# Two single-byte clears on GpSimd behind every row gather of an edge-attention kernel

## The reference

```python
K, Q, V = typed_linear(x, Wk), typed_linear(x, Wq), typed_linear(x, Wv)   # 192 wide, weights by node type
def edge_msgs(Kn, Qn, Vn, ek, eq):
    k = concat([Kn, ek]).reshape(-1, 4, 56);  q = concat([Qn, eq]).reshape(-1, 4, 56)
    att = einsum('ehd,ed->eh', k, q.sum(axis=1)) / sqrt(56)
    return att, concat([Vn, ek]).reshape(-1, 4, 56)
att, v     = edge_msgs(K[row], Q[col], V[row], e1, e2)      # pass o = 0, edges sorted by destination
att_i, v_i = edge_msgs(K[col], Q[row], V[col], e2, e1)      # pass o = 1, edges sorted by source
att, att_i = seg_softmax(att, col), seg_softmax(att_i, row)
agg = segment_sum([v * att, e0], col) + segment_sum([v_i * att_i, e0], row)
```

## Time and profile before

| | us |
|---|---|
| median of 3 runs (lowest to highest) | 4512.24 (4508.96 to 4513.65) |
| the profiled execution | 4514.77 |
| its span in the trace | 4513.0 |
| score pass 0, first gather to last product (L1436) | 1998.13 to 2696.44 |
| score pass 1, first gather to last product (L1436) | 3066.69 to 3773.75 |
| POOL busy over the whole span | 2876.4 (64%) |
| PE, DVE, ACT busy | 63%, 53%, 38% |

### The profile page before, as it was taken

How to read it: one execution, slowest core, us unless ns; L and a number is a source line. 1 busy time by engine, 2 the same in 40 slices (tenths; PEclk the granted TensorE clock), 3 DMA queues, 4 the chain that set the end, 5 groups by cost and what they waited for, 6 DMA issues and landing times.

```text
span 4513.0 us, 51523 instructions
## 1 busy us (share of the span) xinstructions
PE 2845.5 (63%) x13735; PEld 1923.5 (43%) x13735; DVE 2409.3 (53%) x5005; ACT 1721.4 (38%) x4345; POOL 2876.4 (64%) x2661
## 2 busy tenths in 40 slices
PE   4200005545473990767777778996777777996698
PEld 1000003333362660224444447884444445885455
DVE  6434434444451114336777775556777776665353
ACT  2222310000021112125555556774555555885451
POOL 4777776666667887665555557996555553555640
PEclk5555556777785995777777778997777778997798
DMA  5444449333345653677676676777887765664300
GB/s 163 134 136 127 141 116 245 91 93 93 89 90 191 196 183 101 212 220 215 202 212 207 203 191 163 204 193 190 208 210 208 209 203 141 173 173 131 102 1 29
DMA packets 805880, 720.83 MB, mean 160 GB/s; under 512 B 424290, under 2 KB 700364, under 8 KB 805469
## 3 DMA queue, kind: packets, MB, share of 16 engines
q1 hardware_dynamic: 645116, 399.08, 31.1%
q0 software_dynamic: 153536, 315.11, 25.1%
q10 hardware_dynamic: 6944, 3.34, 0.3%
HBM read 482.09 MB, written 241.99 MB: 160 GB/s over the span
## 4 chain that ended last, share of the span: by engine, by line
DVE 20%; POOL 16%; another core or an unknown queue 12%; PE 12%; issue 9%; ACT 7%; DVEq 4%; ACTq 2%; DMA 1%; SPq 1%; POOLq 0%
POOL rec_src L564 9%; DVE META L1423 7%; POOL AR L1661 4%; DVE BIGR L648 3%; DVE AR L1443 3%; ACT AR L1717 2%; DVEq L1439 2%; DVE AR L639 2%; DVE AR L1436 2%; ACT AR L1719 1%; ACT AR L1547 1%; PE ps L1822 1%; PE ps L2433 1%; ACTq L1718 1%
## 5 line engine op out<-in xcount | busy, mean ns | idle before, releaser
L1392 POOL DMA_INDIRECT AR<-kv_tab,META x832 | 791.0, 951 | 599.8 <-DVE AR L1436 337.0
L536 POOL DMA_INDIRECT rec_dst<-AR,slot_e x400 | 484.6, 1211 | 166.7 <-issue 166.4
L1423 DVE TENSOR_REDUCE META<-ps 128x8 f32<-128x1024 f32 x416 | 507.7, 1221 | 97.9 <-remote 57.7
L668 PE MATMUL ps<-AR 128*128 128x256 f32 x832 | 305.6, 532 | 362.4 <-issue 151.0
L622 POOL DMA_INDIRECT AR<-xn_tab,META x416 | 397.9, 956 | 199.7 <-issue 128.6
L1661 POOL TENSOR_TENSOR AR<-AR 128x896 f32<-128x896 f32 x208 | 352.1, 1693 | 233.3 <-ACT AR L1726 230.4
L1626 DVE TENSOR_TENSOR BIGR<-BIGR,ps 128x260 f32 x832 | 353.6, 425 | 228.9 <-PE ps L1700 144.6
L1700 PE MATMUL ps<-AR 128*128 128x260 f32 x1664 | 419.5, 395 | 11.3 <-POOL AR L1661 5.4
L1521 PE MATMUL ps<-AR,identb 128*128 128x512 bf16 x832 | 405.4, 487 | 15.4 <-issue 8.5
L564 POOL DMA_INDIRECT rec_src<-AR,slot_e x290 | 351.8, 1213 | 91.8 <-issue 88.3
L668 PEld LDWEIGHTS ps<-AR 128*128 128x128 f32 x832 | 212.8, 268 | 456.1 <-issue 262.3
(11 more groups left out here) (432 smaller groups left out, 5815.7 us busy)
## 6 DMA issues: line engine op xcount, KB each, us to landing
v_dst<-AR SPq DMA_DIRECT2D x104, 384.0 KB
AR<-v_dst SPq DMA_DIRECT2D x104, 384.0 KB
v_src<-AR SPq DMA_DIRECT2D x104, 384.0 KB
AR<-v_src SPq DMA_DIRECT2D x104, 384.0 KB
AR<-in_W_qvk SPq DMA_DIRECT2D x44, 608.0 KB
rec_raw<-AR SPq DMA_DIRECT2D x40, 640.0 KB, 3.3
AR<-rec_dst SPq DMA_DIRECT2D x104, 192.0 KB
AR<-rec_src SPq DMA_DIRECT2D x104, 192.0 KB
```

Source lines behind the costliest of these rows:

```text
L536: pool.indirect_dma_start(rec_tab[0], bass.IndirectOffsetOnAxis(ap=slot_e[0][0:EP, c * CC + k:c * CC + k + 1].bitcast(U32), axis=0), RD[s] ...
L668: ins = pe.matmul(l0_ps(s, u), OW[s][:, u, :], GA[s][:, u, :], start=True, stop=True)
L1392: pool.indirect_dma_start(KVR[s][:, u, 0:KV], None, kv_tab, bass.IndirectOffsetOnAxis(ap=META[o][:, g * U + u, 0:1].bitcast(U32), axis=0)) ...
L1423: ve.tensor_reduce(BMALL[o][:, g * U + 2 * half:g * U + 2 * half + 2, :].rearrange("p b h -> p (b h)"), PSA[:, 2048 + 1024 * half:3072 + 1 ...
```

## The change

Behind each of the 416 gathers of a pass POOL now executes two `memset` instructions, each of which writes a zero into one column of one byte on all 128 partitions of a new tile `PAD` (128 x 832 bytes). Gather b writes columns 2b and 2b+1, so no column is written twice within a pass. Nothing reads `PAD`. A `drain` closes the function. The rest of the kernel is unchanged, and all four other engines have the same instruction lists as before.

```diff
@@ -108,6 +108,7 @@
         ttype = sb("ttype", [1, TT], I32)
+        PAD = sb("PAD", [P, 832], mybir.dt.uint8)
@@ -1392,6 +1393,10 @@
                     pool.indirect_dma_start(KVR[s][:, u, 0:KV], None, kv_tab,
                                             bass.IndirectOffsetOnAxis(ap=META[o][:, g * U + u, 0:1].bitcast(U32), axis=0)
                                             ).then_inc(sem(f"rows{s}"), 16)
+                    for k in range(2):
+                        b = 2 * (g * U + u) + k
+                        pool.memset(PAD[:, b:b + 1], 0.0)
+            pool.drain()
```

## The result

The changed kernel took 4530.06 us (median of 7 runs, 4522.87 to 4533.44) against 4512.24 us of the kernel before; the ratio is **1.0031, 95% interval [1.0016, 1.0045]** (the quotient of the two medians, 1.0039, lies within it). One of the seven executions of the kernel before that ran beside it took 5703.81 us and is not part of the ratio. The forecast was 4350 us, faster. The profiled execution took 4523.49 us, its span is 4521.8 us.

The account below looks back on a forecast made before the run. The score passes were taken as bound by a loop: lagging gathers delay PE's signals, so product and slots are late and POOL stops. 4514.8 - 186 (no late signals) + 20 (pauses) = 4349, said as 4350 us; range 4285 to 4605.

Parts of the forecast that it names:

- x: Time the two clears add from one POOL gather to the next: taken as 0.16 us, ends -0.03 and 0.26.
- the sum: Score passes: 6.65 - 5.7 = 0.95 us saved per group, some 196 of 208 groups, 186 us; 20 us of pauses off.
- edge: Gathers issued every 1.26 us, worked off every 1.41: the backlog grows 0.15 us each unless x makes up the difference.
- lag: Gathers worked off more slowly than POOL issues them, 0.15 us more behind each; PE's signals held back after five or six.
- rate of 1.41 us: Time per gather at which gathers are worked off, against 1.26 us at issue; gathers 1.42 us apart would avoid late signals.
- Rival 1 with 4: Score passes: blocks of eight stay and POOL's idle time hides the clears, 4505 to 4523 us; chance 0.13, rival 4 included.
- rival 4: Clears run beside the gather, gathers stay 1.26 us apart, no change in time; counted within the joint chance of 0.13.
- Rival 2: Score passes: block stays, its end hangs on the last gather; 4600 us at x = 0.16, 4525 at 0.06; chance 0.22.
- Rival 3: Clears cost more than any row says, POOL becomes the bound from x = 0.41; 4700 us at x = 0.62; chance 0.10.

Follow-up runs that it names:

- 260 columns: Changed kernel with one 260-column clear behind each gather instead of two single-column clears, no closing drain: 4395.56 us, 0.9724 of the kernel before.
- 130 columns: Changed kernel with one 130-column clear behind each gather instead of two single-column clears, no closing drain: 4490.85 us, 0.9946 of the kernel before.
- clears at the end: Changed kernel with its 1664 clears and two drains moved behind all other POOL work: 4520.65 us, 1.0006 of the kernel before (1.0000 where that took 4085.72 us).
- 230 columns: Changed kernel, one 230-column clear behind each gather, no closing drain: 4488.86 us (0.9878 of the kernel before), or 4207.90 us (1.0299) in the faster chip condition.

## Why the prediction was wrong, point by point

- **The size of x: here it failed.** The prediction added an overlapped end of 0.06 us and a serial one of 0.26 us and took the middle, 0.16, "as neither row shows a short instruction between two gathers". x is 0.00 (timeline), and within 0.005 of it over 832 gathers where POOL sets the end. So the gathers stayed 1.26 us apart, the runs stayed at eight, and the whole gain of 186 us that the sum books had nothing to come from. The gap of 0.30 us between two gathers isn't a fixed toll that follows whatever was last. It is 0.16 us that stay ahead of any gather, and 0.14 us in which POOL can do something else, and two clears of a column take exactly these. The bounds did hold the value. The middle between them was no estimate, and it lay on the far side of the prediction's own edge, x = 0.15.
- **What the Trainium skill said of it.** The page Perfetto Trace Analysis, section GPSIMD Engine Instruction, has GpSimd timed by the spacing of starts. The trace agrees: 101 to 147 ns are shown for a clear, two of them fill 0.14 us, and start to start of the gathers nothing changed. The prediction had this as its first rival and weighed it too low.
- **What bounds the kernel: held in part.** That POOL's pauses hang on PE's late signals held: moving the gathers apart by 0.20 us removed the pauses and 2.8%, and in the condition in which no signal is late the kernel takes 4086 us. What failed is the picture behind it. The transfers don't lag (they land 2.4 us after their start, the 24th of a row like the first, and nothing moves in the last 2.4 us ahead of the signal), and the signals are late at a distance at which no lag should build up (359.6 us on ACT with 260 columns). That 260 columns gain near what was forecast for such a distance is thus no proof of the mechanism. What holds PE's signals back stays open.
- **The rate of 1.41 us: a description, no edge.** It was read as the slope between runs of 8 and 24 gathers, "a straight line". Rows of 12, 20 and 32 gathers at the start of the L0 pass of the same trace take 16.48, 27.53 and 44.18 us to the late signal, 0.6 to 1.1 us less than the line gives. The averages of the L0 pass are 1.426 to 1.441 us, standstills included. Distances of 1.35, 1.43 and 1.46 us gained 0.5, 1.2 and 2.8%, without a jump at 1.41.
- **The gain from a given x: somewhat high.** By its own working 260 columns (5.83 us a group) would be 4512 - (6.65 - 5.83) x 196 + 20 = 4371 us. Measured 4395.56 against 4519.17, so 124 us against 141. The late signals of ACT did not go (359.6 us against a forecast "go"); only POOL no longer stopped for them.
- **The drains: a price without a row.** The prediction put a drain at 0.2 us at most. One in each group cost 2.6 us. The two of the changed kernel fall into idle time, so this did no harm to the forecast.
- **Rival 1 with 4, at 0.13, was the outcome**: gathers 1.26 us apart (rival 4), clears inside POOL's idle time, blocks and period as before, 4505 to 4523 us. The time came out 7 us above its end, at 4530. **Rival 2** forecast 4525 us for a small x, which is near by luck, as the 130 columns refute its mechanism. **Rival 3** (POOL becomes the bound) is what happens to wide clears without lag, not to these.
- **The 0.3%.** None of the cases had it, and the prediction put the extra instruction bytes and PAD at nothing. It shows in the condition with lag alone, and the clears' place is its likelier main cause. In the traces the median period of a run of eight goes from 13.28 to 13.30 us (kernel before, two traces, two passes each) and 13.29 and 13.31 (clears at the end) to 13.33 to 13.35 (changed kernel, four passes): 0.05 us times some 80 runs is 4 us of the 12 to 18. The rest lies in longer pauses and in a stage ahead of the passes: the last scatter of L1300 starts at 1993.8 and 1996.3 us in the two traces of the kernel before, and at 2001.7 and 2001.5 us in the two of the changed one. But it starts at 2001.9 with the clears at the end too, which is hardly slower as a whole, so that one trace of a kernel doesn't settle where 10 us lie. How a clear in an idle gap makes a block 0.05 us longer stays open, and so does the cause of the 0.3% as a whole.

The range of 4285 to 4605 us held the time because it was wide enough for outcomes on both sides of no change; the forecast and its sign did not hold.

## What to carry to other kernels

An edge that decides (here x = 0.15) deserves a row of its own: find the gap into which the added work can go, before its price is worked out, and don't take the middle of two bounds that lie on either side of the edge. When engines wait for a releaser "remote" during rows of GpSimd gathers, issuing more slowly can be faster; test it by spacing the issue, and test it in both conditions of the chip, since 230 columns that won 1.2% in one lost 3.0% in the other. Before a queue is called the cause, look whether it is busy while the others wait: one window over the wait would have shown the DMA engines idle. Order two writes of GpSimd by a count that is long reached, not by a drain among indirect transfers.

## What the runs showed of the hardware that I had not expected

- The same kernel took 4086 us in some sets and 4510 to 4550 us in others, with the same durations of instructions (953 ns for a gather of the L0 pass). The L0 pass took 1.26 us per gather in the one and 1.43 to 1.44 us in the other, standstills included, while its gathers landed 2.4 us after their start in both.
- With lag, PE's signal reached DVE at 1029.66 us after 2.4 us in which no engine worked and DMA moved nothing.
- The releaser "remote", 457.3 us ahead of ACT's copy in the recorded trace, is absent without lag, where the same waits read "PE".
- Between two gathers of GpSimd some 0.14 us of other GpSimd work are free; a clear lasts 0.22 us at 130 columns of bytes, 0.31 at 230, 0.33 at 260 and 0.98 at 1040, and what exceeds the free part shows fully in the distance of the gathers (0.09, 0.17, 0.20 and 0.85 us).
- A drain on GpSimd behind four indirect gathers cost 2.6 us, and the next gather started 1.3 us after the fourth had landed.
